# Another order of the steps in the third phase of a two-layer decoder kernel on one core

## The reference

```python
x = x + attn(layernorm(x), w_qkv, w_proj)            # 16 causal heads of width 16
x = x + xattn(ctx, layernorm(x), mask, ...)          # 8 heads of width 64
x = x + ternary_ffn(layernorm(x), weight)            # rows rounded to 8 bits, weight to -1, 0, 1
# in xattn: c = ln(ctx)*w+b; l = ln(ln(x))*w+b; keys and values from both c and l (256 rows)
# q = l2norm(l @ Wq), k = l2norm([c, l] @ Wk), v = [c, l] @ Wv
# out = layernorm(softmax(8 q k^T, masked) v @ Wo)
```

## Time and profile before

| what | value |
|---|---|
| runs, median (lowest to highest) | 4044.49 us (4042.93 to 4050.74), 3 runs |
| profiled execution | 4028.71 us, of which the profile's span is 4027.1 us |
| busy over the span | PE 3741.4 us (93%), DVE 3082.5 (77%), ACT 2793.7 (69%), POOL 2523.8 (63%) |
| phase 3, first to last Ak | 2093.2 to 3920.2 us, 64 tiles |
| mean granted TensorE clock | 0.973 of full speed |

### The profile page before, as it was taken

One profiled execution on the slowest core, in us unless ns is written; L12 is line 12 of the kernel. 1 busy time (PEld: TensorE's weight loads), 2 busy tenths in 40 slices (PEclk: granted clock), 3 DMA queues, 4 the chain that ended last, 5 costly groups with the idle time before them and its releaser, 6 DMA issues.

```text
span 4027.1 us, 119475 instructions
## 1 busy us (share of the span) xinstructions
PE 3741.4 (93%) x34582; PEld 2920.7 (73%) x34583; DVE 3082.5 (77%) x8792; ACT 2793.7 (69%) x8434; POOL 2523.8 (63%) x3252
## 2 busy tenths in 40 slices
PE   5999999999999999979978999999999999999997
PEld 4888888888888888867755666666666666666664
DVE  5888888888888888845546777777777777777775
ACT  4778777778888788844436666767667666766764
POOL 4566655656666566622236777777777777777774
PEclk8999999999999999979989999999999999999998
DMA  4334432333333333324420111111011111111110
GB/s 132 134 116 125 137 123 95 115 116 100 111 117 117 116 108 108 113 74 146 144 90 26 34 32 31 34 31 34 28 33 32 32 33 31 34 30 31 32 30 17
DMA packets 222650, 304.24 MB, mean 76 GB/s; under 512 B 57216, under 2 KB 176256, under 8 KB 222592
## 3 DMA queue, kind: packets, MB, share of 16 engines
q1 hardware_dynamic: 197632, 249.83, 19.5%
q0 software_dynamic: 19200, 52.45, 4.0%
q10 hardware_dynamic: 5760, 1.24, 0.2%
HBM read 239.18 MB, written 64.23 MB: 75 GB/s over the span
## 4 chain that ended last, share of the span: by engine, by line
PE 39%; issue 21%; DVE 16%; POOL 10%; ACT 9%; DVEq 2%; DMA 1%; ACTq 1%; POOLq 0%; SPq 0%
PE Q L1553 10%; PE Q L1546 8%; PE Q L1558 5%; PE Q L1933 3%; PE Q L1779 3%; PE Q L1587 3%; POOL arena L673 2%; DVE mx L1135 2%; PE Q L1791 2%; ACT arena L1348 2%; POOL arena L681 1%; ACT arena L1345 1%; PE Q L1874 1%; POOL arena L678 1%; ACT arena L1342 1%
## 5 line engine op out<-in xcount | busy, mean ns | idle before, releaser
L1558 PE MATMUL Q<-ident,arena 128*128 128x128 f32 x3488 | 587.5, 285 | 109.8 <-ACT arena L1282 34.3
L1558 PEld LDWEIGHTS Q<-ident,arena 128*128 128x128 f32 x3488 | 408.3, 143 | 350.0 <-issue 168.3
L1553 PE MATMUL Q<-Wkvl,arena 128*128 128x512 f32 x1024 | 520.8, 601 | 1.5 <-ACT arena L1497 0.8
L673 POOL TENSOR_TENSOR arena<-arena 128x1024 f32<-128x1024 f32 x256 | 481.6, 1902 | 37.0 <-DMA arena<-cum_rows 36.7
L744 POOL TENSOR_TENSOR l<-l,half_pow 128x8 f32<-128x8 f32 x192 | 317.5, 1654 | 146.0 <-DVE l L1154 145.9
L1466 ACT ACTIVATE arena<-Q,mx 128x128 f32<-128x128 f32 x1024 | 359.8, 386 | 6.2 <-DVE mx L1135 6.2
L1381 ACT ACTIVATE arena<-Q,mx 128x128 f32<-128x128 f32 x1024 | 287.2, 386 | 101.5 <-DVE mx L960 97.3
L1546 PE MATMUL Q<-arena,Win 128*128 128x128 f32 x2560 | 347.6, 280 | 1.3 <-DVE arena L890 1.3
L1587 PE MATMUL Q<-ident,arena 128*128 128x128 f32 x2048 | 322.9, 282 | 22.2 <-ACT arena L1381 12.1
L1546 PEld LDWEIGHTS Q<-arena,Win 128*128 128x128 f32 x2560 | 324.9, 196 | 6.3 <-DVE arena L890 2.0
L914 DVE TENSOR_TENSOR arena<-arena,Q 128x1024 f32<-128x1024 f32 x256 | 311.8, 1218 | 14.0 <-ACT arena L1336 7.0
(11 more groups left out here) (292 smaller groups left out, 10195.7 us busy)
## 6 DMA issues: line engine op xcount, KB each, us to landing
arena<-cum_rows SPq DMA_DIRECT2D x256, 512.0 KB, 6.3
arena<-routed_rows SPq DMA_DIRECT2D x144, 128.0 KB, 2.0
expert_rows<-arena POOLq DMA_DIRECT2D x144, 128.0 KB, 2.0
arena<-in_x_dram SPq DMA_DIRECT2D x128, 128.0 KB, 4.4
arena<-in_ctx_dram SPq DMA_DIRECT2D x128, 128.0 KB, 3.0
x_rows<-arena SPq DMA_DIRECT2D x128, 128.0 KB, 1.7
arena<-x_rows SPq DMA_DIRECT2D x128, 128.0 KB, 2.1
out_dram<-arena SPq DMA_DIRECT2D x64, 128.0 KB, 1.7
```

Of the source, the lines that this page charges most:

```text
L673: tell(g.tensor_tensor(E8[j], E8[j], cums[:, 8 * j:8 * j + 8].unsqueeze(2).broadcast_to([P, 8, T]), ALU.subtract), "diff")
L1553: last = mm(out, lhs(c), rhs(c), start=c == 0, stop=c == n - 1)
L1558: last = nc.tensor.transpose(out[:, c * P:(c + 1) * P], src[:, c * P:(c + 1) * P], ident[:, :])
```

## The change

The strings of `ORDER[3]` are written anew for all five queues. The steps, their instructions, their waits, the chains' lags (how many tiles each lies behind) and the buffers stay as they are. No function is touched. Phases 1 and 2 are the same.

```diff
     3: {
         "SP": """
-            Cc Tx Lm Ax Uo Kx
+            Lm Tx Cc Ax Uo Kx
         "POOL": """
-            Clnc Uln7 Kx4c Ag Kln5 Hlq2 Sp0 Sp1 Clq0 Sp2 Kln6 Sp3 Tlno Aln4 Klq1 Lp0 Lp1 Lp2 Lp3
+            Clnc Uln7 Kx4c Kln5 Ag Hlq2 Sp0 Sp1 Clq0 Kln6 Sp2 Sp3 Aln4 Tlno Klq1 Lp0 Lp1 Lp2 Lp3
         "DVE": """
-            Lmr Clnc Uln7 Rt0 Clncn Kln5 Rt2 Uaq Sm0 Hlq2 Sm1 Ux6 Sm2 Sm3 Sp0 Kln5n Hlu2 Sp1 Clq0 Kln6 Sp2 Clu0 Ax3 Kln6n Sp3 St0 Lm0 Lm1 Tlno Aln4
-            St2 Aln4n Klq1 Lm2 Lm3 Tx5 Lp0 Klu1 Lp1 Lp2 Sx4 Ak Lp3
+            Uln7 Clnc Kln5 Rt0 Clncn Rt2 Uaq Kln5n Sm0 Hlq2 Sm1 Ux6 Sm2 Sm3 Sp0 Hlu2 Sp1 Clq0 Kln6 Clu0 Ax3 Sp2 Lmr Sp3 St0 Kln6n Lm0 Aln4 St2 Lm1
+            Tlno Aln4n Tx5 Klq1 Lm2 Lm3 Lp0 Lp1 Sx4 Klu1 Lp2 Lp3 Ak
         "ACT": """
-            Rt1 Hlq2 Clncn Rt3 UaT Sm0 Sm1 Clq0 Rlo HlT2 Sm2 Sm3 ClT0 Hla4 Kln6n Lp0 Lp1 St1 St3 Klq1 SoT Aln4n Lp2 Lp3 KlT1 Aq Cla3 Ac
+            Rt1 Hlq2 Clncn Rt3 UaT Sm0 Sm1 Clq0 Rlo HlT2 Sm2 Sm3 ClT0 Hla4 Kln6n St1 Lp0 St3 Lp1 Klq1 SoT Aln4n Lp2 Lp3 Aq Ac KlT1 Cla3
         "PE": """
-            Rt0 Hla2 Rt1 Rt2 Hla2h Rt3 Clncn Ss0 UaT Cla1 Utern Cla1h Rpv0 Rpv1 HlT2 St0 Two Hla4 Hla4h St1 ClT0 St2 Ls0 Kln6n Twoh St3 Kla0 Kla0h Ls2
-            Spv Spvh Aln4n Cla3 Spr Aq Aqv Ak KlT1 Cla3h
+            Rt0 Rt1 Hla2 Rt2 Rt3 Clncn Hla2h Ss0 UaT Cla1 Utern Cla1h Rpv0 Rpv1 HlT2 St0 Two Hla4 Hla4h St1 ClT0 Twoh Ls0 Kln6n St2 Cla3 St3 Kla0
+            Kla0h Spv Spvh Ls2 Aln4n Spr Aq Aqv Ak KlT1 Cla3h
```

## The result

| | kernel before | changed kernel |
|---|---|---|
| median (lowest to highest), 6 runs each | 4043.71 us (4042.72 to 4050.74) | 4079.68 us (4071.63 to 4087.13) |
| profiled execution, its span | 4028.71, 4027.1 | 4081.76, 4080.1 |
| phase 3, first to last Ak | 1827.0 us | 1876.4 us |

What follows compares the result with a forecast made beforehand. The prediction took a cycle through DVE, POOL, ACT and PE as the bound; its stretches summed to -0.04 us a tile, times 60 = -2.4 us, forecasting 4042 us with the carried 15.8; range 4021 to 4063.

Steps and rivals of the forecast that it cites:

- Ak to Sp0: First stretch of the loop body, on DVE: four terms, -0.08 - 0.21 + 0.39 + 0.44, summing to +0.54 us a tile.
- Sp0 to Ls0: Second stretch, through POOL, DVE and ACT: POOL's first multiplication gets shorter with Kln5n gone from beside it, -0.15 us.
- Ls0 to Ak: Third stretch, on PE: loses Twoh (0.87) and gains St2 (0.44), -0.43 us a tile.
- Second and third stretch: The body from Sp0 to Ls0, claimed at -0.15 us, and from Ls0 to the next Ak, claimed at -0.43.
- Cla3's move: PE, third stretch: Cla3 no longer covers ACT's copy of the transposed norm; it just fits, 0, bound +0.13 us.
- Kln5n +0.39: DVE, first stretch: Kln5n, until now behind Sp0, is brought in and costs +0.39 us.
- The stall at Rt2, +0.44: DVE, first stretch: Rt2 waits for PE's transposes, starting 1.44 behind Rt0 instead of 1.00; bounds 0 and 0.5.
- L1230: DVE, first stretch: kept at 0.53 us; the faster rival had it at 0.29, -0.24 a tile more, chance 0.28.
- Lmr and L654: Slower rivals on DVE: Lmr beside POOL, +0.68 a tile, chance 0.08; Uaq held by L654, +24 us, chance 0.08.
- Other queues: Moves on SP, ACT, POOL and DVE's Klu1, each priced at 0, among them Ag about 0.9 us later on POOL.
- The signs of being wrong: A new wait on PE between Ls0 and Ak, or no DVE idle time before the second L1200.
- I carry the difference over: Whole kernel: the median's 15.8 us above the profiled execution was added to 4026.3, giving 4042.

Runs made afterwards that it cites:

- e1: The kernel before, unchanged, profiled again on a chip of the first kind: 4012.46 us, ratio 0.9989 to the kernel before.
- e2: The changed kernel, unchanged, run again on a chip of the first kind: 4006.39 us, ratio 0.9974 to the kernel before.
- e5: The kernel before, unchanged, profiled on a chip of the second kind: 4040.44 us, ratio 0.9997 to the kernel before.
- e12: The changed kernel, unchanged, run on a chip of the second kind: 4072.57 us, ratio 1.0086 to the kernel before.
- e8_twoh: The kernel before with only PE's Twoh and St2 changing places about Ls0: 4013.71 us, ratio 0.9991 to the kernel before.
- e9_kln5n: The kernel before with only DVE's Kln5n moved ahead of Sm0, from behind Sp0: 4074.33 us, ratio 1.0138 to the kernel before.
- e3_hla2h: The changed kernel with PE's Hla2h moved directly behind Hla2, ahead of Rt2: 4026.82 us, ratio 1.0036 to the kernel before.
- e10_ss0: The changed kernel with PE's Ss0 put back ahead of Hla2h: 4193.10 us, ratio 1.0390 to the kernel before.
- e11_cover2: The changed kernel with DVE's Kln5 put between Rt0 and Clncn: 4075.93 us, ratio 1.0084 to the kernel before.
- e6_after: The changed kernel, unchanged, once more on another chip of the first kind: 4006.86 us, ratio 0.9976 to the kernel before.
- e7: The changed kernel with DVE's Kln5 put back between Clncn and Rt2: 4015.08 us, ratio 0.9997 to the kernel before.
- e15: The kernel before with only PE's order from Twoh to Spr as in the changed one: 4094.73 us, ratio 1.0177 to the kernel before.
- e17_plain: The changed kernel with Ag's two indirect DMAs replaced by plain DMAs of fixed rows: 4008.82 us, ratio 0.9921 to the kernel before.

## Why the prediction was wrong, point by point

The prediction's sum was +0.54 - 0.15 - 0.43 = -0.04 us a body. Measured, from the medians above:

| stretch | predicted | first kind (e1 to e2) | second kind (e5 to e12) | profile before to profile after |
|---|---|---|---|---|
| Ak to Sp0 | +0.54 | +0.41 | +1.16 | +1.46 |
| Sp0 to Ls0 | -0.15 | -0.15 | -0.14 | -0.15 |
| Ls0 to Ak | -0.43 | -0.43 | -0.43 | -0.43 |
| sum | -0.04 | -0.16 | +0.59 | +0.88 |

- **Second and third stretch: right**, on every chip. The first L739 took 1.04 in the median, Twoh covered PE's wait at Ls0 (3058.24 has none), and Cla3's move cost nothing. Why Cla3's own new place mattered, as cover of ACT's copies of Kln6n, I had not seen; e8_twoh showed that without it 0.29 of the 0.43 would have been lost.
- **Kln5n +0.39: right** (3032.13 to 3032.53 in e2_after, no wait), but only because POOL's Kln5 was moved ahead of Ag at the same time; alone it costs 0.95 (e9_kln5n).
- **The stall at Rt2, +0.44: right in kind and in size.** Rt2 starts 1.44 behind Rt0 (3042.34 to 3043.78), as forecast. The idle time of 0.36 is less than the cost of 0.44, since the stall also takes away the 0.08 by which instructions back to back overlap. e3_hla2h made the idle time 0.64 by moving the transposes, as the mechanism has it.
- **L1230: the rival was right in kind**, 0.35 where I kept 0.53 and it said 0.29. On the first kind of chip this 0.17 is what parts +0.41 from +0.54, with 0.04 the other way. In all runs with indirect DMAs L1230 took 0.29 where it started 0.56 us or more ahead of such a DMA's end, and lasted to 0.1 behind the end where it started 0.24 to 0.47 ahead of it (0.35 to 0.55; medians): 0.2 us decides.
- **Lmr and L654: rightly given little.** L1185 took 0.263 in the median and 0.284 at most. Uaq's first instruction met L654 and took 0.405 in the median, as in the kernel before; the Trainium skill's exclusive lock (SBUF — State Buffer, "SBUF: two separate sides") did not show for a power of one column here either.
- **The step that failed** is in "Other queues": "POOL: Ag about 0.9 later, its rows wanted 8 us after: 0." I priced a moved DMA by when its data are wanted. Its price is what it does to others while POOL carries it out: on the chips of the second kind the completions of Ss0 that fall due in it come only behind its end. Later by 1.3 in the body and not by 0.9, it covers the moment at which Ss0 is done, and Sm0 waits 0.95, until 0.5 behind it. Set against the profile before, which has no such wait, this is 1.04 of the 1.46 (8.48 against 7.44 for Sm0); the other 0.42 is the stretch as it is on the first kind. That Ag's place alone makes this difference was not run on a chip of the second kind; it is read from the release, which keeps to the second DMA's end in e10_ss0, e11_cover2 and the result while Ss0's own end moves by 1.0.
- **The signs of being wrong did not cover this.** Both that I named, a new wait of PE behind Ls0 and no idle time before the second L1200, stayed away, and "the change cannot fail to do what it says: each queue is in order" was too sure: a new wait at Sm0 was not on the list.
- **The other error was of the base.** "I carry the difference over": the 15.8 us between the profiled execution and the median were a sign that the runs paid for something the trace did not show. The kernel before pays 0.3 a body on the second kind, 18 us over 60. That the gap of 15.8 is this and nothing else is my reading; it was not tested.

On the first kind the forecast would have come out a little low on the gain: -0.16 times 60 is -10 us, and e2_after and e6_after measured -9. There the change is the faster by 0.25%; on the second kind it is slower by 0.85%.

## What to carry to other kernels

A step moved past a DMA issue is not priced until you know what the issue does to the other engines while it runs: look where completions land relative to it, and take traces from more than one chip before the sign of a 0.2% change is believed. In a woven order a step has two values, its own time and the latency that it covers; moving it alone gives neither (e7, e8, e9 and e15 all lost what the whole change kept). When profile and median of one kernel differ by more than the runs' spread, ask why before summing.

## What the hardware showed that I had not expected

- On chips of the second kind the consumer of Ss0's result, done during POOL's indirect DMAs, starts 0.3 to 0.5 us behind the end of the second (0.51 in the result, 0.34 in e11_cover2; 0.49 on ACT for Hla2h in e10_ss0), even where the matmuls ended 1.8 us before that end (e11_cover2: 3075.10 against 3076.86). On the first kind Sm0 starts without a wait while the second is still running (e2_after). With plain DMAs from the same queue the wait is gone (e17_plain), though these do not overlap Ss0's end on POOL. Three chips of the experiments were of each kind. What differs between them is not known.
- The row of a matmul shows little of this. In e11_cover2 Ss0 takes 1.11 as on the first kind and only the waiting engine's idle time tells; in the result it takes 1.48, and in e5_before it has a gap. The Trainium skill (Perfetto Trace Analysis, "Tensor Engine Instruction (MATMUL, LD_WEIGHTS)") says that the profiled end of a matmul is an estimate and that the completion is sent after the results are acknowledged. The trace agrees in so far as 1.3 us lie between the two here. Whether the matmuls or only their completions are late in that time, these rows can't tell.
- The Trainium skill (Trainium Architecture — The Big Picture, "What this means for kernel authors") says that the engines are independent and that a matmul doesn't block a copy on VectorE unless a semaphore stands between them. On the second kind the measurement differs: POOL's indirect DMA delayed DVE's start on PE's result, 0.95 us a body, with no dependency between the DMA and either.
